# Six tiles of a crossed-feature lookup moved from gathers to TensorE, and a weight load moved forward

## The reference: what is computed

```
VOCABS = [125000, 25000, 12500, 375, 375, 1000, 500, 100]
wide = dense @ Wd_wide                                  # dense: 2048 x 13
for si, wi in zip(S, w): wide = wide + wi[si]           # eight single weights
wide = wide + wc0[S[3] * VOCABS[4] + S[4]]              # first crossed table, 375 * 375 entries
wide = wide + wc1[S[5] * VOCABS[6] + S[6]]              # second crossed table, 1000 * 500 entries
deep_in = concat([dense @ Wd_deep] + [Ei[si] ...], 1)   # 9 * 64 columns
h = relu(deep_in @ W1)                                  # 512 columns
h = relu(h @ W2)                                        # 256 columns
y = bias + h @ W3 + wide
```

## Time and profile before

| | |
|---|---|
| median of three runs | 137.04 us (136.63 to 137.73) |
| profiled execution, device time | 137.18 us |
| profiled execution, span from its first to its last instruction | 135.3 us |
| instructions | 1728 |
| TensorE matmul busy | 112.7 us (83%) |
| TensorE weight loads busy (beside the matmuls) | 83.4 us (62%) |
| GpSimd busy | 110.9 us (82%) |
| VectorE busy | 71.7 us (53%) |
| ScalarE busy | 55.0 us (41%) |
| mean granted TensorE clock | 0.938 of full speed |

### The profile page before, as it was taken

How to read it: one execution, slowest core, us unless ns; L and a number is a source line. 1 busy time by engine, 2 the same in 40 slices (tenths; PEclk the granted TensorE clock), 3 DMA queues, 4 the chain that set the end, 5 groups by cost and what they waited for, 6 DMA issues and landing times.

```text
span 135.3 us, 1728 instructions
## 1 busy us (share of the span) xinstructions
PE 112.7 (83%) x588; PEld 83.4 (62%) x588; DVE 71.7 (53%) x163; ACT 55.0 (41%) x97; POOL 110.9 (82%) x157
## 2 busy tenths in 40 slices
PE   6979999929779999999999999999999999920000
PEld 2544875726566886687888858878886788920000
DVE  2696984822399905868980166999304019310000
ACT  3698946131925224248261515456242325210000
POOL 5587877999899999989999989999998998989800
PEclk9999999995999999999999999999999999995555
DMA  4958436868632232223323320000000000000000
GB/s 138 306 115 277 29 66 28 218 122 224 207 27 22 20 26 22 20 20 20 25 19 26 22 20 0 0 0 0 5 0 0 1 0 0 5 0 0 0 3 0
DMA packets 6096, 6.90 MB, mean 51 GB/s; under 512 B 2931, under 2 KB 4115, under 8 KB 6088
## 3 DMA queue, kind: packets, MB, share of 16 engines
q0 software_dynamic: 2560, 1.62, 15.8%
q1 hardware_dynamic: 3096, 4.45, 10.8%
q10 hardware_dynamic: 432, 0.72, 1.5%
HBM read 6.60 MB, written 0.19 MB: 50 GB/s over the span
## 4 chain that ended last, share of the span: by engine, by line
POOL 79%; issue 11%; DMA 4%; DVE 1%; POOLq 1%; DVEq 0%
POOL x_pair L289 25%; POOL cross L307 21%; POOL pause_sb L282 21%; POOL x_two L297 12%; DMA idx_raw<-in_index_dram 2%; DMA cross<-in_wc_dram,idx_cross 2%; POOLq L80 1%; DVE idx_wrap L443 0%; DVE idx_sum L445 0%; DVE idx_look L448 0%; DVE result L606 0%; DVE idx_gather L448 0%; DVEq L605 0%
## 5 line engine op out<-in xcount | busy, mean ns | idle before, releaser
L463 DVE TENSOR_SCALAR onehot<-idx_bc,row_id 128x512 fp32r<-128x512 f16 x76 | 39.5, 586 | 4.7 <-PE io_ps L646 1.9
L289 POOL DMA_INDIRECT x_pair<-in_rows_dram,idx_gather x32 | 33.3, 1041 | 8.5 <-issue 6.2
L307 POOL DMA_INDIRECT cross<-in_wc_dram,idx_cross x32 | 30.9, 965 | 5.3 <-issue 5.3
L282 POOL MEMSET pause_sb<- 128x320 f32 x67 | 29.0, 434 | 0.0
L663 PE MATMUL l_ps<-xt_hi,w_hi 128*128 128x512 f32 x64 | 25.6, 400 | 0.0
L665 PE MATMUL l_ps<-xt_hi,w_lo 128*128 128x512 f32 x64 | 25.1, 392 | 0.0
L664 PE MATMUL l_ps<-xt_lo,w_hi 128*128 128x512 f32 x64 | 25.0, 391 | 0.0
L634 PE MATMUL io_ps<-onehot,table_hl 128*128 128x512 f32 x76 | 21.9, 414 | 0.2
L483 DVE TENSOR_TENSOR xt_lo<-io_ps,xt_hi 128x512 fp32r<-128x512 f32 (+1 forms) x8 | 5.5, 687 | 28.4 <-ACT xt_hi L339 27.5
L326 ACT CAST xt_hi<-io_ps 64x512 fp32r<-64x512 f32 x20 | 11.6, 579 | 19.8 <-PE io_ps L634 18.9
L297 POOL DMA_INDIRECT x_two<-in_rows_dram,idx_gather x16 | 16.1, 1004 | 3.2 <-issue 3.2
(11 more groups left out here) (75 smaller groups left out, 106.8 us busy)
## 6 DMA issues: line engine op xcount, KB each, us to landing
idx_bc<-idx_dram SPq DMA_DIRECT2D x3, 640.0 KB, 4.9
w_sb<-in_w_dram ACTq DMA_DIRECT2D x2, 256.0 KB
x_pair<-in_rows_dram,idx_gather POOLq DMA_INDIRECT x32
w_sb<-in_w_dram SPq DMA_DIRECT2D x2, 256.0 KB
w_sb<-in_w_dram SPq DMA_DIRECT2D x1, 512.0 KB
cross<-in_wc_dram,idx_cross POOLq DMA_INDIRECT x32
dense_stack<-dense_dram SPq DMA_DIRECT2D x3, 156.0 KB
table<-in_small_dram SPq DMA_DIRECT2D x1, 416.0 KB
```

Source lines behind the costliest of these rows:

```text
L282: nc.gpsimd.memset(pause_sb[:], 0.0).then_inc(paused, 1)
L289: nc.gpsimd.indirect_dma_start(out=x_pair[:, t, g * ROW:(g + 1) * ROW], out_offset=None, in_=big[g], in_offset=bass.IndirectOffsetOnAxis(a ...
L307: nc.gpsimd.indirect_dma_start(out=cross[:, c, t:t + 1], out_offset=None, in_=wc[c], in_offset=bass.IndirectOffsetOnAxis(ap=idx_cross[:, c ...
L463: nc.vector.tensor_scalar(onehot[:, CHUNK0[i] + c, :], idx_bc[:, b, i, :], row_id[:, c:c + 1], None, ALU.is_equal).then_inc(onehot_ready, 1)
```

## The change

There are two parts.

**Crossed table 0, tiles 0 to 5.** They are no longer gathered. The 375 x 375 table is loaded to SBUF (into the place of the small tables, once these are split), as three chunks of 128 rows by 376 columns, and split in hi and lo. The crossed index is divided into row and column (`cross_indices`, now ahead of `build_onehot(1, 0)`). TensorE spreads the rows over the partitions (`spread_row`), VectorE makes one-hots of them, three for each pair of tiles (`build_row_onehot`), TensorE picks each sample's table row in six products of 376 columns (`look_up_crossed`), and VectorE masks the sample's column and sums (`take_crossed`). One tile comes behind `layer1(b, 2)` and one behind `layer1(b, 0)` in each of blocks 1 to 3. Ten gathers are left for table 0, sixteen for table 1.

**W2** is loaded behind the index spread of block 1 and ahead of the dense part, into the buffer of W1's last two groups; ScalarE rounds it ahead of `turned_hi(0, 0)`. On VectorE its low part comes ahead of `turned_lo(0, 1)`, and the one-hots for `look_up(1, 2)` and `look_up(1, 3)` ahead of `relu_lo(0, ...)`. On TensorE `dense(0)` comes ahead of `turn(0, 1)`.

To make room, `idx_bc` has three buffers instead of four, and `wide_look`, `h2_first` and `h2_w3` become one pair `wide_deep_look`, for which ScalarE waits on `deep_done`.

```diff
+IO_ORDER += [("look", 1, 0)] + [("spread_row", q, 0) for q in range(len(XGROUPS))]
+IO_ORDER += [("turn", 0, 1), ("look", 1, 1)]
+def crossed(b, half):
+    return [t for t in range(XTILES) if (t // 2 + 1, t % 2) == (b, half)]
...
@@ SP
             spread_block(1)
...
+            sp.wait_ge(index_spread[1], 16)
+
+            sp.wait_ge(w1_low, 2)
+            sp.dma_start(w2_sb, w2.rearrange("(k p) n -> p k n", p=P)).then_inc(w2_loaded, 16)
             sp.wait_ge(dense_last, 1)
...
-            sp.dma_start(w2_sb[:], w2.rearrange("(k p) n -> p k n", p=P)).then_inc(w2_loaded, 16)
...
+            sp.wait_ge(table_low, len(GROUPS))
+            sp.dma_start(cross_table, wc_rows).then_inc(cross_table_loaded, 16)
+            sp.wait_ge(onehot_ready, NCH)
             for b in range(2, BLOCKS):
                 spread_block(b)
@@ GpSimd
+            nc.gpsimd.iota(col_id[:], pattern=[[1, XPAD]], base=0, channel_multiplier=0,
...
             for c in range(NX):
-                for t in range(TILES):
+                for t in range(XTILES if c == 0 else 0, TILES):
@@ ScalarE
             weight_high(1)
+            act.wait_ge(w2_loaded, 16)
+            nc.scalar.copy(w2_hi[:], w2_sb).then_inc(w2_high, 1)
             turned_hi(0, 0)
...
             looked(1, 0)
+            for q in range(len(XGROUPS)):
+                copy_row(q)
             turned_hi(0, 1)
             looked(1, 1)
-            act.wait_ge(w2_loaded, 16)
-            nc.scalar.copy(w2_hi[:], w2_sb[:]).then_inc(w2_high, 1)
             for b in range(BLOCKS):
                 for m in range(M1):
                     relu1(b, m)
+                if b == 0:
+                    act.wait_ge(cross_table_loaded, 16)
+                    nc.scalar.copy(cross_hl[:, 0], cross_table).then_inc(cross_high, 1)
@@ VectorE
+            def build_row_onehot(q):
...
+                for c in range(XCHUNKS):
+                    nc.vector.tensor_scalar(row_onehot[:, c, :], row_bc[:, 2 * q * P:2 * (q + 1) * P],
+                                            row_id[:, c:c + 1], None, ALU.is_equal).then_inc(row_onehot_ready, 1)
+            def take_crossed(t):
...
+                nc.vector.scalar_tensor_tensor(out=taken[:], in0=col_id[:], scalar=cross_col[:, t:t + 1],
+                                               in1=io_bank(use)[:, 0:XPAD], op0=ALU.is_equal, op1=ALU.mult,
+                                               accum_out=cross[:, 0, t:t + 1]).then_inc(io_dve, 1)
...
+            cross_indices()
             build_onehot(1, 0)
             build_onehot(1, 1)
             w1_low_part(3)
+            weight_low(w2_lo[:], w2_sb, w2_hi[:], w2_high, 1, w2_low)
             turned_lo(0, 1)
-            weight_low(w2_lo[:], w2_sb[:], w2_hi[:], w2_high, 1, w2_low)
+            build_onehot(1, 2)
+            build_onehot(1, 3)
             for b in range(BLOCKS):
                 for m in range(M1):
                     relu_lo(b, m)
+                for t in crossed(b, 1):
+                    take_crossed(t)
+                    if t + 1 < XTILES:
+                        build_row_onehot((t + 1) // 2)
                 if b == 0:
-                    build_onehot(1, 2)
-                    build_onehot(1, 3)
+                    dve.wait_ge(cross_high, 1)
+                    nc.vector.tensor_tensor(cross_hl[:, 1], cross_table, cross_hl[:, 0].bitcast(f32),
+                                            ALU.subtract).then_inc(cross_low, 1)
+                    build_row_onehot(0)
                 if b + 1 < BLOCKS:
                     build_onehot(b + 1, 4)
                     weigh_first(b)
+                    for t in crossed(b + 1, 0):
+                        take_crossed(t)
                     turned_lo(b + 1, 0)
@@ TensorE
+            def look_up_crossed(t):
...
+                for c in range(XCHUNKS):
+                    for part in range(2):
+                        last = nc.tensor.matmul(io_bank(use)[:, 0:XPAD], row_onehot[:, c, t % 2 * P:(t % 2 + 1) * P],
+                                                cross_hl[:, part, c, :], start=c + part == 0,
+                                                stop=c + part == XCHUNKS)
...
             look_up(1, 0)
+            spread_row(0)
+            dense(0)
+            for q in range(1, len(XGROUPS)):
+                spread_row(q)
             turn(0, 1)
-            dense(0)
...
                 layer1(b + 1, 2)
+                for t in crossed(b + 1, 0):
+                    look_up_crossed(t)
                 layer2(b, 1)
...
                 layer1(b + 1, 0)
+                for t in crossed(b + 1, 1):
+                    look_up_crossed(t)
```

More of the change, by code:

```diff
@@ L48 @@
 BUSY = [4, 5]
+XROWS, XCOLS = VOCABS[CROSSES[0][0]], VOCABS[CROSSES[0][1]]
+XPAD = XCOLS + XCOLS % 2
+XCHUNKS = -(-XROWS // P)
+XTILES = 6
+XGROUPS = [range(t, min(t + BT, XTILES)) for t in range(0, XTILES, BT)]
+ROUND = 1.5 * 2.0 ** 23
 IO_ORDER = [("spread", 0, i) for i in range(NL)] + [("look", 0, i) for i in range(4)]
 IO_ORDER += [("turn", 0, 0), ("look", 0, 4), ("wide", 0, 0)]
-for _b in range(BLOCKS):
-    if _b > 0:
-        IO_ORDER += [("look", _b, i) for i in (2, 3, 4)] + [("turn", _b, 0), ("wide", _b, 0)]
+IO_ORDER += [("look", 1, 0)] + [("spread_row", q, 0) for q in range(len(XGROUPS))]
+IO_ORDER += [("turn", 0, 1), ("look", 1, 1)]
+def crossed(b, half):
+    return [t for t in range(XTILES) if (t // 2 + 1, t % 2) == (b, half)]
+for _b in range(1, BLOCKS):
+    IO_ORDER += [("look", _b, 2), ("look", _b, 3)] + [("crossed", t, 0) for t in crossed(_b, 0)]
+    IO_ORDER += [("look", _b, 4), ("turn", _b, 0), ("wide", _b, 0)]
     if _b + 1 < BLOCKS:
-        IO_ORDER += [("look", _b + 1, 0), ("turn", _b, 1), ("look", _b + 1, 1)]
-IO_ORDER += [("turn", BLOCKS - 1, 1)]
+        IO_ORDER += [("look", _b + 1, 0)]
+    IO_ORDER += [("turn", _b, 1)] + [("crossed", t, 0) for t in crossed(_b, 1)]
+    if _b + 1 < BLOCKS:
+        IO_ORDER += [("look", _b + 1, 1)]
 IO_AT = {use: k for k, use in enumerate(IO_ORDER)}
 IO_BANKS = 2
-ACT_OPS = {"spread": 1, "look": 2, "wide": 1, "turn": 1}
-DVE_OPS = {"spread": 0, "look": 0, "wide": 0, "turn": 1}
+ACT_OPS = {"spread": 1, "look": 2, "wide": 1, "turn": 1, "spread_row": 1, "crossed": 0}
+DVE_OPS = {"spread": 0, "look": 0, "wide": 0, "turn": 1, "spread_row": 0, "crossed": 1}
 def act_count(k):
@@ new lines, in build_row_onehot @@
+            def build_row_onehot(q):
+                if q == 0:
+                    for k in range(len(XGROUPS)):
+                        dve.wait_ge(io_act, act_count(IO_AT["spread_row", k, 0]))
+                else:
+                    dve.wait_ge(io_full, IO_AT["crossed", 2 * q - 1, 0] + 1)
+                for c in range(XCHUNKS):
+                    nc.vector.tensor_scalar(row_onehot[:, c, :], row_bc[:, 2 * q * P:2 * (q + 1) * P],
+                                            row_id[:, c:c + 1], None, ALU.is_equal).then_inc(row_onehot_ready, 1)
@@ L660, in turn, with spread_row @@
                 last.then_inc(io_full, 1)
+            def spread_row(q):
+                use = ("spread_row", q, 0)
+                if q == 0:
+                    pe.wait_ge(cross_row_ready, 1)
+                io_free(use)
+                for k, t in enumerate(XGROUPS[q]):
+                    last = nc.tensor.matmul(io_bank(use)[:, k * P:(k + 1) * P],
+                                            cross_row[:, t:t + 1].to_broadcast([P, P]), ident16[:],
+                                            start=True, stop=True)
+                last.then_inc(io_full, 1)
+            def look_up_crossed(t):
+                use = ("crossed", t, 0)
+                io_free(use)
+                if t == 0:
+                    pe.wait_ge(cross_low, 1)
+                if t % 2 == 0:
+                    pe.wait_ge(row_onehot_ready, XCHUNKS * (t // 2 + 1))
+                for c in range(XCHUNKS):
[3 more added lines that the diff above has]
+                                                stop=c + part == XCHUNKS)
+                last.then_inc(io_full, 1)
             def product(dst, w_hi, w_lo, a_hi, a_lo, start, stop):
@@ L719, in layer3 @@
                     t = b * BT + at // P
-                    last = nc.tensor.matmul(deep_ps[:, 0, t:t + 1], h2_w3[:, at:at + P], ones[:],
+                    last = nc.tensor.matmul(deep_ps[:, 0, t:t + 1], wide_deep_look[b % 2][:, at:at + P], ones[:],
                                             start=True, stop=True)
@@ L837 @@
     program(nc, one("index"), one("dense_t"), [one(f"rows{f}") for f in GATHERED], one("small"),
-            one("small_w"), [one(f"wc{c}") for c in range(NX)], one("wd_rep_t"), one("wd_wide"), one("w1"), one("w2"),
+            one("small_w"), [one(f"wc{c}") for c in range(NX)], one("wc_rows"), one("wd_rep_t"), one("wd_wide"), one("w1"), one("w2"),
             one("w3"), one("bias"), out)
```

82 lines of the change are left out of this document (56 added, 26 removed).

## The result

Median device time 129.57 us (129.13 to 132.28, four runs) against 137.33 us for the kernel before on the same chip: ratio 0.943, 95% interval 0.936 to 0.950. The profiled execution took 129.13 us with a span of 127.3 us. Ratios here leave out runs over 1.5% above the fastest of the same kernel; medians and ranges are of all runs.

The account below looks back on a forecast made before the run. GpSimd was taken to be 9.8 us later than TensorE; with 6.5 added, 4.6 gained and 0.5 for W2, TensorE would decide by a hair, result 7.2 us earlier: 129.8 us, range 127.9 to 133.2.

Parts of the forecast that it names:

- GpSimd, six steps, 9.0 us: Gather stretch: six steps of 1.50 us go, so the last gather lands at 120.8 instead of 129.84.
- The doubt: GpSimd's pauses take 0.55 instead of 0.38 us beside one-hots; for nine new ones at most 1.5 us.
- The 5.1 us worked out by that rule: GpSimd locked out for each of nine whole one-hots, 9 x 0.57 us; the sum did without it.
- TensorE, what is added, 6.5 us: Six crossed tiles behind 38 us: 36 products of 0.17 us, 6.1, plus 0.4 for seams, all on the path.
- TensorE's head, 4.6 us: Gain ahead of layer2(0, 0) and look_up(1, 2): 2.9 + 1.0 + 0.7 us, bounds 3 and 5.2.
- W2's new place, 0.5 us: W2's earlier load slows the gathers of block 0 that TensorE waits for: 0 to 2.1 us, taken as 0.5.
- The sum: TensorE's side 122.5 us for wide_deep, GpSimd's 120.9 to 122.4; result 7.2 us earlier, 129.8 us device time.
- The clean head: Rival: cheap table products or full head gain, W2 free, GpSimd decides; 128.1 us, chance 0.12.
- collision: Rival: W2 makes block 0's gathers 2.1 us later, turn(0, 0) stands, clock falls; 132.4 to 133.3 us, chance 0.16.
- VectorE's take: take_crossed on VectorE, which masks and sums each crossed tile: about 0.5 us, with nobody waiting for it.
- What would show it: Signs in the changed trace: last link ahead of result is deep_ps or, within a microsecond, the last gather; start near 122.7.

Follow-up runs that it names:

- run 5: Changed kernel with GpSimd pauses of 192 instead of 320 columns and 13 more memsets behind the last gather: 135.05 and 153.58 us.
- run 9: Changed kernel, pauses still 320 columns, with 12 more memsets behind GpSimd's last gather: 135.83 us, ratio 0.991 to the kernel before.
- run 6: Changed kernel with the index spreads of blocks 2 and 3 issued behind the gathers of block 1: lowest 129.8 and 130.0 us, ratio 0.950.
- run 2: Kernel before with only the W2 and order part, all 32 crossed gathers kept: 140.46 us, ratio 1.018 to before.
- run 1: Changed kernel with only the crossed part, W2 and the order as before: three runs 131.0 to 131.5 us, the fourth 128.97.
- run 4: Changed kernel with the scratch tile of GpSimd's pauses 192 instead of 320 columns wide: 125.06 us, ratio 0.908 to before.
- run 3: Changed kernel with three instead of six products per crossed tile, the table's low part left out: 129.77 us, ratio 0.936 to before.
- run 10: Changed kernel, pauses of 320 columns, with dense(0) behind turn(0, 1) again: lowest 128.88 and 129.16 us, two others 131.9 and 135.4.
- run 11: Changed kernel with each crossed tile's six products made twice: 137.3 us, lowest run 133.62.
- run 7: Changed kernel with pauses of 192 columns and dense(0) behind turn(0, 1) again: 131 to 140 us.

## Why the prediction was right, point by point

The number was right, 129.8 against 129.57, and the range held it; the account of which engine decides was not.

- **GpSimd, six steps, 9.0 us.** 7.5 came, and 0.5 more behind the last gather (runs 5 and 9), which no term had. The doubt was right in size (up to 1.5) and wrong in the place: nine more one-hots left the mean pause at 0.437 against 0.434, and long issues of gathers took the 1.5 us. They stand beside new work of VectorE (run 6), so the doubt may have been right in kind. By the rule that VectorE's two-port mode locks GpSimd out (the Trainium skill, SBUF — State Buffer, "SBUF: two separate sides") both would wait. The traces agree where a pause takes 0.55 beside one-hots, or 3.53 beside eight of them, and not in most gathers, which keep their 0.95. The 5.1 us worked out by that rule took 0.57 us for a one-hot of 256 columns, which by the prediction's own estimate takes half.
- **TensorE, what is added, 6.5 us.** 6 x 1.03 = 6.2; the seams cost nothing, and a product of 376 columns takes the 0.17 us of the interpolation. The 0.4 us allowed for the seams was not needed.
- **TensorE's head, 4.6 us.** `turn(0, 1)` at 28.82 (said: 28.8), `layer2(0, 0)` at 33.99 (34), the five products of `look_up(1, 2)` and `look_up(1, 3)` in 1.33 us, `dense(0)` in 1.02 at full clock. The sum is as worked out: 6.2 - 1.5 = 4.7. In run 2, without the crossed part, the same reordering gave 5.3.
- **W2's new place, 0.5 us.** W2 landed at 19.2 (said: 19.0) and cost TensorE nothing in the changed kernel. GpSimd had one issue of 2.12 us beside W2's load, but the next gather was issued at 19.11, as before (19.12). Alone (run 2) the part made GpSimd 3.8 us later, mostly by a long gather and a long pause that stand beside one-hots, not beside the load.
- **The sum: the step that failed.** "Only then does VectorE add the result (129.93), and 5.37 us of store and end follow" took the tail for a constant behind `result`. Behind `result` it is 2.0 us; the 5.37 were GpSimd's own tail, 6.3 to 6.9 us from the end of its last instruction to the end of the span (run 9, and its DRAIN in every profile; the 2.0 us in runs 1 and 4). So before, GpSimd was late against TensorE not by 9.8 us but by 135.3 - (120.3 + 2.0) = 13.0, and the changed kernel is still bound by GpSimd, with 3.5 us of room on TensorE (runs 3, 10), where the prediction had it that "the bound passes to TensorE, by a hair". Two errors cancelled: my TensorE side was 7.2 us earlier than the end before, GpSimd's real side 8.0 (7.5 and a tail 0.5 shorter). That the two lie so close, and the number with them, is luck.
- **The rivals.** "The clean head" was what happened to TensorE, and GpSimd decided as it said; its 128.1 us lacked GpSimd's long issues. No collision: `turn(0, 0)` came at 19.44, before at 19.55. VectorE's take is 0.6 us, and nobody waited for it.
- **What would show it.** The last link was named as `deep_ps` "or, within a microsecond, the last gather"; it was the gather, by 0.72 us, and this closeness hid 3.5 us of room.

## What to carry to other kernels

Ask of each engine when the program could end if that engine were the last, with what follows behind it: what lies between the last instruction shown and the end of the span can belong to another engine than the one in the chain. A change that moves work from the bound engine to one with room can carry a second part that is worth nothing, and worth less than nothing alone, until the bound has passed. Pauses that look like waste are measured by taking some away, on more than one chip.

## What the runs showed of the hardware that was not expected

- Behind GpSimd's last instruction, gather or memset, its closing DRAIN went on for 6.12 us in programs with 74 gathers, 6.44 with 78 and 6.61 with 80, some 0.083 us for each, and the span ended 0.2 us later; behind the start of `result` with its store it ended after 2.0 us.
- Single GpSimd instructions lasted as long as VectorE worked beside them without a gap: a pause of 0.38 us took 3.53 beside eight one-hots (run 2) and 2.33 beside five (run 6). Most did not, and what decides is open.
- With pauses of 64 columns between indirect gathers ScalarE, VectorE and TensorE stood still for up to 29.6 us with no release that the trace names. With 192 it was up to 6.6 (run 5; none in run 4), with 256 3.1, and with 320 up to 4.2 (run 9; 3.9 in run 11, none in the changed kernel's own profile). What they wait for is open.
- A granted clock of 0.50 (the 1.2 GHz level) followed waits of TensorE of 2.62 us (before), 2.02 us (run 1) and 1.38 and 0.37 us (run 10); behind the waits ahead of `turn(0, 1)` in the changed kernel (0.17 and 0.37 us) and in runs 1 and 7 (1.04 and 0.37) it stayed at 1.00.
